# A fused cross-attention and mixture-of-experts kernel: the norm of batch 29 goes ahead in GpSimd's queue, the logits take four matmuls in place of six, the last tiles get a bank each, and the first context is loaded ahead of the weights

## The reference, cut to what matters

```python
# x (32, 112, 256), ctx (32, 375, 128), 16 heads of 64, 14 routed experts (top 2), 2 shared experts
x = x + tanh(g_xattn) * xattn(layernorm(x), ctx)      # softmax(q k^T / 8) v, then Wo and bo
h = layernorm(x)                                      # all 3584 tokens
def ffn(h, rw, W1, W2):
    return silu((h * rsqrt(mean(h*h) + RMS_EPS) * rw) @ W1) @ W2
gates = softmax(h @ router_w)                         # 14 logits for each token
masked = top2(gates) / (sum(top2) + 1e-9)
routed = sum_e masked[:, e] * ffn(h, rms_w[e], w1[e], w2[e])
shared = sum_e ffn(h, rms_w_s[e], w1_s[e], w2_s[e])
out = x + tanh(g_ffn) * (routed + shared)
```

## Time and profile before

| what | value |
|---|---|
| median of 3 runs | 1454.03 us (1454.0 to 1455.53) |
| profiled execution, its own time | 1453.46 us |
| its span, first to last instruction | 1451.9 us |
| TensorE busy | 1433.0 us, 99% of the span |
| VectorE, ScalarE, GpSimd busy | 74%, 64%, 32% |
| mean granted TensorE clock | 0.998 of full speed |

### The profile page before, as it was taken

How to read it: one execution, slowest core, us unless ns; L and a number is a source line. 1 busy time by engine, 2 the same in 40 slices (tenths; PEclk the granted TensorE clock), 3 DMA queues, 4 the chain that set the end, 5 groups by cost and what they waited for, 6 DMA issues and landing times.

```text
span 1451.9 us, 29493 instructions
## 1 busy us (share of the span) xinstructions
PE 1433.0 (99%) x9774; PEld 1346.5 (93%) x9774; DVE 1081.6 (74%) x2614; ACT 935.3 (64%) x2398; POOL 458.0 (32%) x688
## 2 busy tenths in 40 slices
PE   7999999999999999999999999998999999999998
PEld 6999999999999999999999999998789988888888
DVE  4878888888888888888798888877587544444448
ACT  6777777777777777777777777776453445454552
POOL 4313142231323313143131422326100145555520
PEclk9999999999999999999999999999999999999999
DMA  4010312303112131212303112150022356562235
GB/s 126 7 52 18 116 75 55 103 24 117 75 50 82 50 109 50 84 75 57 109 16 118 75 50 95 36 194 31 28 102 116 131 179 236 212 236 92 77 123 222
DMA packets 55794, 138.02 MB, mean 95 GB/s; under 512 B 10512, under 2 KB 38176, under 8 KB 52064
## 3 DMA queue, kind: packets, MB, share of 16 engines
q1 hardware_dynamic: 49024, 118.01, 23.6%
q0 software_dynamic: 6624, 18.13, 4.0%
HBM read 86.69 MB, written 49.43 MB: 94 GB/s over the span
## 4 chain that ended last, share of the span: by engine, by line
PE 94%; DVE 2%; issue 1%; ACT 1%; POOL 1%; DMA 1%; SPq 0%; ACTq 0%; POOLq 0%
PE bank L589 18%; PE bank L590 18%; PE bank L591 18%; PE bank L650 9%; PE bank L1720 7%; PE bank L1047 6%; PE bank L1039 5%; PE bank L1743 4%; PE bank L1747 2%; PE bank L1731 2%; PE bank L1705 1%; PE bank L1223 1%; PE bank L605 1%; DMA under_wq<-in_Wq 0%; POOL keep_w_in L1149 0%
## 5 line engine op out<-in xcount | busy, mean ns | idle before, releaser
L765 ACT ACTIVATE prob<-bank,nmax 128x375 f32<-128x375 f32 x448 | 258.8, 578 | 183.1 <-DVE nmax L874 181.1
L857 DVE TENSOR_TENSOR pT_lo<-bank,pT_hi 125x384 fp32r<-125x384 f32 x448 | 245.8, 549 | 31.6 <-ACT pT_hi L776 30.1
L874 DVE TENSOR_REDUCE nmax<-bank 128x1 f32<-128x375 f32 x448 | 240.9, 538 | 24.6 <-PE bank L591 24.1
L650 PE MATMUL bank<-keep_ident,prob 128*125 128x128 f32 x1344 | 221.3, 273 | 0.0
L776 ACT CAST pT_hi<-bank 125x384 fp32r<-125x384 f32 x448 | 212.6, 475 | 1.7 <-PE bank L650 1.7
L650 PEld LDWEIGHTS bank<-keep_ident,prob 128*125 128x125 f32 x1344 | 201.9, 187 | 5.7
L589 PE MATMUL bank<-attend_wvo_hi,zT_hi 128*112 128x256 f32 x512 | 169.6, 331 | 0.1
L589 PE MATMUL bank<-attend_kvT_hi,qp_hi 128*128 128x376 f32 x448 | 151.3, 338 | 4.6 <-ACT prob L765 4.5
L589 PE MATMUL bank<-pT_hi,kv_hi 125*128 125x448 f32 x384 | 152.9, 398 | 2.8 <-DVE zT_lo L857 1.3
L590 PE MATMUL bank<-attend_kvT_hi,qp_lo 128*128 128x376 f32 x448 | 150.2, 335 | 0.0
L591 PE MATMUL bank<-attend_kvT_lo,qp_hi 128*128 128x376 f32 x448 | 149.5, 334 | 0.0
(11 more groups left out here) (238 smaller groups left out, 3715.5 us busy)
## 6 DMA issues: line engine op xcount, KB each, us to landing
w_split<-we_split SPq DMA_DIRECT2D x14, 2048.0 KB, 7.4
keep_weights<-w_split SPq DMA_DIRECT2D x14, 2048.0 KB
we_in<-in_w SPq DMA_DIRECT2D x28, 512.0 KB, 6.1
keep_y_all<-y_rows SPq DMA_DIRECT2D x14, 512.0 KB, 8.9
kv_in<-in_ctx SPq DMA_DIRECT2D x32, 187.5 KB
h_rows<-hrow SPq DMA_DIRECT2D x32, 112.4 KB, 2.6
keep_h_in<-h_rows SPq DMA_DIRECT2D x7, 514.0 KB, 9.6
x_in<-in_x SPq DMA_DIRECT2D x16, 224.0 KB, 3.0
```

Source lines behind the costliest of these rows:

```text
L650: last = nc.tensor.transpose(turn_bank_of(s)[0:MP, c * P:(c + 1) * P], prob[:, s % NB, c * MP:(c + 1) * MP], ident[:])
L765: nc.scalar.activation(prob[:, s % NB, :], score_bank(s)[:, 0:M], ACT.Exp, bias=nmax[:, s % NB:s % NB + 1], accum_out=psum_[:, s % NB:s % ...
L857: return nc.vector.tensor_tensor(dst, src, hi.bitcast(F32), ALU.subtract)
L874: nc.vector.tensor_reduce(nmax[:, s % NB:s % NB + 1], score_bank(s)[:, 0:M], AX, ALU.max, negate=True).then_inc(max_ready, 1)
```

## The change

Six edits in one:

1. POOL's queue in pair 15: `scale_shared(1)` is cut in two. The order becomes: all of expert 0, the w1 half of expert 1 (`scale_half`), `ln2_root(29)`, `add_bias(15, 1)`, the w2 part of expert 1 (`scale_rest`), then the splits. Each `scaled(s)` is two steps later than before, the one ahead of `scale_rest(1)` four.
2. SP loads the context of batch 0 ahead of `wk`; PE turns it first of all (`side(-1, KV0)` ahead of the six `turn`), ACT and DVE split it first too.
3. The table load at line 817 is dropped; the one at line 797 stays.
4. `logits`: the high and the low part of the router's weights lie side by side, so that one matmul makes hi·hi and lo·hi as 28 rows, and a second adds hi·lo to the first 14: four matmuls a group in place of six. `turn_logits` becomes four plain fp32 matmuls against a 28x14 matrix of two identities one above the other (`sum_parts`, made once by DVE), which turns and adds the two halves.
5. In `shared_after`, group 6 uses four banks (4 to 7), one for each tile; its first output waits until DVE has added group 5 (`acc_done` 4). PE reports each tile of the last item by itself.
6. The last store of 256 KB is cut into two of 128 KB.

```diff
@@ attend: sync, gpsimd
             weights["sync_gates"](sp)
             load_x(0)
+            load_kv(0, 0)
             weights["sync_keys"](sp)
-            load_kv(0, 0)
             weights["sync_values"](sp)
...
-            sb["scale_shared"](pool, 0, lambda: scaled(4), lambda: scaled(6))
+            sb["scale_shared"](pool, 0, lambda: scaled(6), lambda: scaled(8))
+            sb["scale_half"](pool, 1, lambda: scaled(10))
+            ln2_root(2 * p - 1)
             add_bias(p, 1)
-            sb["scale_shared"](pool, 1, lambda: scaled(8), lambda: scaled(10))
-            ln2_root(2 * p - 1)
+            sb["scale_rest"](pool, 1, lambda: scaled(14))
             pool.wait_ge(side_done, job_index(p, Q[7]) + 1)
-            sb["split_shared"](pool, 0, lambda: scaled(14), lambda: scaled(16), lambda: scaled(18))
-            sb["split_shared"](pool, 1, lambda: scaled(20), lambda: scaled(22), lambda: scaled(24))
+            sb["split_shared"](pool, 0, lambda: scaled(16), lambda: scaled(18), lambda: scaled(20))
+            sb["split_shared"](pool, 1, lambda: scaled(22), lambda: scaled(24), lambda: scaled(26))
@@ attend: tensor (scalar and vector likewise)
+            weights["wait_identity"](pe)
+            side(-1, KV0)
             for i in range(6):
                 weights["turn"](pe, i)
...
             side(-1, Q2)
-            side(-1, KV0)
             side(-1, Q3)
@@ attend: scalar
-            nc.scalar.preload_act_table_set("natural_log_exp_and_others")
             for p in range(PAIRS):
@@ front: logits, turn_logits, split_router
-            for n, (k, (w, h)) in enumerate((k, q) for k in range(2) for q in PRODUCTS):
-                last = nc.tensor.matmul(lt_bank(g)[0:E, :], rwp[w][:, k, :], hT_of(sb, h, g)[:, k, :],
-                                        start=n == 0, stop=n == 5)
+            for k in range(2):
+                nc.tensor.matmul(lt_bank(g)[0:2 * E, :], rw_split[:, k, :, :].rearrange("p q e -> p (q e)"),
+                                 hT_of(sb, "hi", g)[:, k, :], start=k == 0, stop=k == 1, skip_group_check=True)
+                last = nc.tensor.matmul(lt_bank(g)[0:E, :], rwp["hi"][:, k, :], hT_of(sb, "lo", g)[:, k, :],
+                                        start=False, stop=k == 1, skip_group_check=True)
...
+                if g == 0:
+                    pe.wait_ge(sum_ok, 1)
                 for t in range(4):
-                    last = nc.tensor.transpose(l_bank(g)[:, t * E:(t + 1) * E], logitT[:, b, t * P:(t + 1) * P],
-                                               sb["ident"][0:E, 0:E])
+                    last = nc.tensor.matmul(l_bank(g)[:, t * E:(t + 1) * E], logitT[:, b, t * P:(t + 1) * P],
+                                            sum_parts[:, :], start=True, stop=True)
...
+            nc.vector.tensor_tensor(sum_parts[:], sb["ident"][0:2 * E, 0:E], sb["ident"][0:2 * E, E:2 * E], ALU.add
+                                    ).then_inc(sum_ok, 1)
@@ shared_after
+        def out_bank(g, t):
+            return O_BANK[t] if g == GROUPS - 1 else O_BANK[2 * (g % 2) + t // 2]
...
-            for t in (0, 2):
-                sp.wait_ge(acc_done, 4 * (g - BEFORE) + t + 2)
-                sp.dma_start(by_group(io["out"], g)[:, t:t + 2, :], acc[:, 4 * g + t:4 * g + t + 2, :]).then_inc(out_stored, 16)
+            for t, n in ((0, 2), (2, 1), (3, 1)):
+                sp.wait_ge(acc_done, 4 * (g - BEFORE) + t + n)
+                sp.dma_start(by_group(io["out"], g)[:, t:t + n, :], acc[:, 4 * g + t:4 * g + t + n, :]).then_inc(out_stored, 16)
...
+                alone = items[i][0] == GROUPS - 1
+                if alone and e == 0:
+                    pe.wait_ge(acc_done, 4)
                 for t in range(4):
-                    last = shared_output(nc, sb, hid, e, t, O_BANK[2 * (items[i][0] % 2) + t // 2])
-                    if t % 2:
+                    last = shared_output(nc, sb, hid, e, t, out_bank(items[i][0], t), alone)
+                    if t % 2 or i == len(items) - 1:
                         last.then_inc(o_done, 1)
```

More of the change, by code:

```diff
@@ L121, in turn @@
             if i == 0:
-                pe.wait_ge(ident_ok, 1)
                 pe.wait_ge(wk_in, 16)
@@ L128, in turn @@
                 pe.wait_ge(whole_ok, 2)
-                pe.wait_ge(sb["side_lo"], 3)
+                pe.wait_ge(sb["side_lo"], 4)
             for j, src in enumerate(turn_sources[i][1]):
@@ L139, in fuse @@
                     pe.wait_ge(fused_lo, 4)
+                if i == 0:
+                    pe.wait_ge(sb["side_lo"], 1)
                 if i == 7:
-                    pe.wait_ge(sb["side_lo"], 2)
+                    pe.wait_ge(sb["side_lo"], 3)
             else:
@@ L210, in fuse_weights @@
         return {"sync_gates": sync_gates, "sync_keys": sync_keys, "sync_values": sync_values, "gpsimd": gpsimd,
-                "gpsimd_bias": gpsimd_bias, "turn": turn, "fuse": fuse, "copy_turned": copy_turned, "tanh": scalar_tanh,
+                "gpsimd_bias": gpsimd_bias, "wait_identity": lambda pe: pe.wait_ge(ident_ok, 1), "turn": turn, "fuse": fuse, "copy_turned": copy_turned, "tanh": scalar_tanh,
                 "split_hi": split_hi, "split_lo": split_lo, "copy_whole": copy_whole, "split_four": split_four}
@@ L313, in job_index @@
         def job_index(p, k):
+            if isinstance(p, int) and p == -1:
+                return (1, 2, 3, 4, 0, 5)[k - OWN]
             return NJ * p + k + NJ - OWN
@@ L320, in side_bank @@
         def side_bank(p, k):
-            return banks[(6, 3, 6, 7, 0, 1)[k - OWN]] if isinstance(p, int) and p < 0 else SIDE
+            return banks[(6, 3, 6, 7, 7, 1)[k - OWN]] if isinstance(p, int) and p < 0 else SIDE
         FUSED_AT = {s: (6 + 2 * s, 7 + 2 * s) for s in range(1, 5)}
@@ L1041, in shared_hidden, with shared_output @@
     return last
-def shared_output(nc, sb, hid, e, t, bank):
+def shared_output(nc, sb, hid, e, t, bank, alone=False):
+    half = 0 if alone else t % 2
     for n, (j, (h, w)) in enumerate((j, q) for j in range(4) for q in PRODUCTS):
-        last = nc.tensor.matmul(bank[:, (t % 2) * D:(t % 2 + 1) * D], hid[h][:, e, j, t * P:(t + 1) * P],
-                                sb["w2s_" + w][:, e, j, :], start=e == 0 and t % 2 == 0 and n == 0,
-                                stop=e == SHARED - 1 and t % 2 == 1 and n == 11, skip_group_check=True)
+        last = nc.tensor.matmul(bank[:, half * D:(half + 1) * D], hid[h][:, e, j, t * P:(t + 1) * P],
+                                sb["w2s_" + w][:, e, j, :], start=e == 0 and half == 0 and n == 0,
+                                stop=e == SHARED - 1 and (alone or half == 1) and n == 11, skip_group_check=True)
     return last
@@ L1068, in front @@
         rw = buf("rw", [P, 2, E])
-        rwp = {q: buf("rw_" + q, [P, 2, E], F32R) for q in ("hi", "lo")}
+        rw_split = buf("rw_split", [P, 2, 2, E], F32R)
+        rwp = {q: rw_split[:, :, i, :] for i, q in enumerate(("hi", "lo"))}
+        sum_parts = buf("sum_parts", [2 * E, E])
         logitT, logit, prob, tie, scan1 = sb["logitT"], sb["logit"], sb["gate_prob"], sb["tie"], sb["scan1"]
@@ L1150, in scale_shared, with scale_rest @@
                                         ).then_inc(w_step, 1)
+        def scale_rest(pool, e, wait_second):
             wait_second()
             nc.gpsimd.tensor_scalar(w2_in[:, e], w2_in[:, e], sb["tanh_g"][:, 1:2], None, ALU.mult).then_inc(w_step, 1)
+        def scale_shared(pool, e, wait_first, wait_second):
+            scale_half(pool, e, wait_first)
+            scale_rest(pool, e, wait_second)
         def split_shared(pool, e, wait_hi, *wait_lo):
@@ L1910, in accumulate @@
                 for t in range(4):
-                    dve.wait_ge(o_done, 2 * i + t // 2 + 1)
+                    dve.wait_ge(o_done, 2 * i + (t if i == len(items) - 1 else t // 2) + 1)
                     dve.wait_ge(y_added, 4 * TOPK * order.index(g) + 4 + t + 1)
-                    out = O_BANK[2 * (g % 2) + t // 2][:, (t % 2) * D:(t % 2 + 1) * D]
+                    half = 0 if g == GROUPS - 1 else t % 2
+                    out = out_bank(g, t)[:, half * D:(half + 1) * D]
                     nc.vector.tensor_tensor(acc[:, 4 * g + t, :], out, acc[:, 4 * g + t, :], ALU.add).then_inc(acc_done, 1)
```

11 lines of the change are left out of this document (6 added, 5 removed).

## The result

The changed kernel takes 1451.27 us (median of 19 runs, 1448.95 to 1453.34) beside 1454.47 us for the kernel before on the same chip (19 runs): ratio 0.9976, 95% interval 0.9970 to 0.9983. The forecast was 1446.4 (1442.8 to 1449.3). The direction was right, the gain is 3.2 us instead of 7.6, and the time lies outside the range.

A forecast was written before the change was run, and what follows sets the result against it. It took TensorE, busy 99% of the span, as the bound. Pair 15 -7.4, start -0.4, logits +0.1 and end +0.1 summed to -7.6 us: 1454.03 to 1446.4 us, range 1442.8 to 1449.3.

The forecast's parts named there:

- The wait in pair 15: Pair 15: PE's waits around the late exponential and the clock lost there would go, -7.4 us, bounds 4.7 to 8.0.
- -7.4 us, all on PE's path: Pair 15: POOL's earlier root ends ACT's wait, work now behind the root is in time, and PE gains the full 7.4.
- That landing moves by 192,000 B / 308 GB/s = 0.6 us: Start: the context's bytes, loaded first, delay the last half of wq by 0.6 us; +0.28 after 0.32 saved on turning.
- The table load: Start: dropping it ends PE's 0.65 us idle before the third scores; with the context's load, -0.4 for both edits.
- That rival: Start: the table load comes back before the first exponential, +0.28 in place of -0.4, 1447.1 us; inside the forecast's 0.68.
- Logits: Routing logits: fewer matmuls save 3.25 us, two-pass fp32 turns at 0.1025 a pass add 3.36; net +0.1, bounds -0.9 to +1.9.
- the rival that they pay: Logits: a 14-column fp32 matmul costs no more than the transpose it replaces, -3.25, 1443.1 us; in full or half 0.20.
- the trace agrees on 128 moving columns: Logits: the trace's 0.1025 us a pass was said to agree with the skill's 107 ns weight-load estimate for 128 columns.
- End: End: PE's new wait with restart +0.75, one add less -0.35, smaller last store -0.35; net +0.1, bounds -0.4 to +0.7.
- a constant 1.56 us: Whole execution: the time around the span, 1.56 us in the profiled execution, was taken over unchanged.
- POOL is still late: Pair 15: expert 1's half starts only at 985.12 as before, half of the 7.4 stays lost, 1450.1 us; chance 0.09.
- the wait at the end grows: End: the four adds come after the routed adds, PE waits 7.1 us and the clock falls, 1456.2 us; chance 0.03.

The follow-up runs named there:

- r1: The changed kernel once more, unchanged; its time is not given directly, but the changed kernel with the old logits, 1449.74 us, is 1.8 us below it.
- e13: The kernel before with only POOL's new order, expert 1's w2 scaling held until after tile 16's normalisation, and the dropped table load; 1447.10 us, ratio 0.9951.
- e4: The changed kernel with POOL's scaling of expert 1's w2 held until after tile 16's normalisation, and the splits one step later; 1449.44 us.
- e14: The changed kernel with POOL's w2 scaling at the same place but cut into two instructions of 512 elements; 1452.61 us.
- e15: The changed kernel with batch 0's context loaded behind wk and ahead of wq, and turned behind wk's turns; time not given, start mark +0.98 us.
- e12: The kernel before with the new logits and nothing else; +2.7 us against the kernel before, ratio 1.0017.
- e9: The kernel before with only its second table load dropped; 1454.40 us beside 1454.65.

## Why the prediction was wrong

- **The wait in pair 15** was sized right: -7.4 forecast, -7.43, -7.34 and -7.04 in r1, e13 and e4. **The step that failed is "-7.4 us, all on PE's path"**: what now stood behind the root on POOL was looked at for being late, and not for what it lies beside on DVE. The scaling, moved from 988.35 to 990.64, lies over the normalisation of tile 16, which then takes 2.03 us in place of 0.42. With six long ones in nine traces the stage is worth about 6.0: +1.4. That POOL's scaling is the cause is shown by e4 and e14; that 2.03 or 0.42 goes with 10 to 30 ns in the distance of the starts is read from the traces, and why is open. It could have been read beforehand: the earlier trace rows have a normalisation of 0.76 us while POOL was scaling, and the trace of the kernel before has the one of tile 18 held to about 1.6 us in fourteen pairs. Which of the two lengths a given distance brings could not.
- **"That landing moves by 192,000 B / 308 GB/s = 0.6 us" failed.** The sum priced the bytes at the mean rate of a later window and looked at `wq` alone. `wk` is what PE waits for first; it came 2.6 us later, and the rate just behind x was 130 GB/s. And the landing that the sum did look at, `wq`'s last half, moved by 1.6 us and not by 0.6, in e15 also with the rate back. The mean start mark of the six traces with the whole new start is +1.19; the five with the old start and one load have -0.35. The order costs 1.5 and not 0.28. That the low rate belongs to the place behind x is shown by e15; the reason for it, and for the rest of `wq`'s lateness, stays open.
- **The table load** was forecast at about -0.65 within that sum and is worth 0.3 (times, within noise) to 0.7 (marks). That rival fell.
- **Logits.** The doubled passes were right, and so was turning down the rival that they pay: 0.118 us a pass where 0.1025 was taken, inside the bounds: 8 x 0.118 = 0.94 a group, and 7 x (0.94 - 0.34) - 3.25 = +0.95. A wait of 0.4 us for `logitT`, which the kernel before has here and the changed one has not, brings it near the +0.7 of the marks. The prediction's remark that the trace agrees on 128 moving columns holds for the pace of a pass, 0.1025 us; the weight load itself takes 188 ns in the earlier trace rows. But no term and no rival had the clock fall behind work. The text watched it only near 990. Five falls in eight traces (four of 1.6, one of 3.2) are 1.2 us on the mean, and e12 puts the whole edit at +2.7. This is the largest single miss, about +1.8.
- **End:** +0.3 for +0.1. PE's wait and restart cost 0.9 (0.75 forecast), and the add and the smaller store gave back 0.33 and 0.35 as forecast. Another 0.3 us are lost outside the span, which the sum held at a constant 1.56 us and which is 1.87 now: 0.13 goes with the dropped load (e9) and about 0.2 with the third store.

The sum with measured sizes: start +0.8 (+1.19 less 0.37, the mean of the three with the old start and two loads), pair 15 -6.0, logits +1.9, end +0.3, outside the span +0.3: -2.7, beside -3.2 measured. The rivals "POOL is still late" and "the wait at the end grows" did not occur: POOL's half of expert 1 begins at 982.38, and ACT takes the root with no wait.

## What to carry to other kernels

Where a step is moved, list what it will lie beside, not only what queues behind it: a long GpSimd instruction can hold a VectorE one until it ends. Starting it behind the tight one cost nothing here (e4, e13); splitting it shortened the hold to 0.76 us in the one trace. Ten nanoseconds in the distance of the two starts can decide, so one profile without the hold does not clear an order. Fewer or smaller matmuls are not cheaper when the ones that stay are tiny and stand in a row, since the clock can fall behind them with PE never idle; put a larger matmul between them. The first transfers of a program set the landing that everything waits for, and their order is worth measuring before it is priced by a mean rate. And an execution's time outside the span is a term too: it changed by 0.3 us here.

## What the runs showed of the hardware that was not expected

- A VectorE `tensor_scalar` of 128 x 375 took 2.03 us instead of 0.42 under a GpSimd `tensor_scalar` of 2.85 us in six of nine traces, with the starts 1.028 to 1.036 us apart in the six and 1.000 to 1.021 in the three. The Trainium skill, page "SBUF — State Buffer", section "Who interferes with whom", has, for a VectorE instruction in one of the modes that use two ports, whichever of the two engines issues first hold a shared port pair for its whole instruction, and the other block. The six traces and e14 agree (the end comes 0.2 us behind GpSimd's); the three with 0.42 us do not follow from it, and neither do the eleven that end 1.32 to 1.33 us into GpSimd's 2.85.
- TensorE's clock fell to 0.50 with no idle time in front of it, within or up to 1.2 us behind 16 fp32 passes of 14 columns, in five of eight traces, for 3.4 us (four times) and 6.8.
- A plain fp32 matmul with 14 moving columns costs two passes of 0.118 to 0.124 us, no less than one with 128 (0.1025).
- With a transfer of 1,536-byte packets directly behind one of 1,024-byte packets, the DMA engines moved 129 to 154 GB/s for two microseconds in seven traces, where they moved 286 to 395 with `wk` in that place (nine traces).
- The first record of a clock of 1.00 stood at 9.6 to 14.6 us in the sixteen traces, and the early marks moved with it by up to 1.7 us among kernels with the same order of loads.
